# A convolution in quarter products with two transfers a pair, and attention denominators inverted once for four chunks

## What is computed

```python
x = x + L0(gn(x))      # linear attention over multi-scale heads
x = x + L1(gn(x))      # sparse plus linear attention, 4 heads of 64

def L0(x):
    qkv = conv1x1(x, w_qkv)                       # 768 channels
    agg = conv5x5_depthwise(qkv, w_dw, pad=2)
    agg = conv1x1(agg, w_pw, groups=96)           # mixes 8 channels of a head
    ms = concat([qkv, agg])                       # 64 heads of (q, k, v), 8 channels each
    q, k = relu(q), relu(k);  v = [v, 1]
    kv = einsum('bgnd,bgne->bgde', k, v)
    out = einsum('bgnd,bgde->bgne', q, kv)
    out = out[..., :-1] / (out[..., -1:] + 1e-15) # the denominators
    return conv1x1(out, w_proj)
```

## Time and profile before

| | |
|---|---|
| median of 3 runs | 9082.88 us (9064.64 to 9105.43) |
| the profiled execution's own time | 9057.69 us |
| its span | 9055.9 us |
| PE, PE weight load | 84%, 57% of the span busy |
| DVE, ACT, POOL | 56%, 39%, 42% |
| mean granted clock of PE | 0.919 of full |

### The profile page before, as it was taken

One profiled execution on the slowest core, in us unless ns is written; L12 is line 12 of the kernel. 1 busy time (PEld: TensorE's weight loads), 2 busy tenths in 40 slices (PEclk: granted clock), 3 DMA queues, 4 the chain that ended last, 5 costly groups with the idle time before them and its releaser, 6 DMA issues.

```text
span 9055.9 us, 206227 instructions
## 1 busy us (share of the span) xinstructions
PE 7636.7 (84%) x65004; PEld 5190.5 (57%) x65004; DVE 5037.9 (56%) x11563; ACT 3520.5 (39%) x9207; POOL 3786.7 (42%) x10084
## 2 busy tenths in 40 slices
PE   8978799787997879978899778997789977799788
PEld 5655556555565555655555555565555555566555
DVE  3475644756447564475644756447564475644655
ACT  1145621445214552145521455215552155511555
POOL 2345533445334553345533444334443344533444
PEclk9988999888999889988999888998889988999888
DMA  3201122011220112201122111221112211122111
GB/s 101 65 16 26 41 87 65 16 26 38 89 65 16 27 42 85 65 18 26 51 75 65 21 22 49 77 65 21 23 53 73 65 22 22 57 68 65 24 20 55
DMA packets 398743, 431.90 MB, mean 48 GB/s; under 512 B 159184, under 2 KB 355984, under 8 KB 393296
## 3 DMA queue, kind: packets, MB, share of 16 engines
q1 hardware_dynamic: 397648, 418.42, 16.3%
HBM read 102.76 MB, written 67.63 MB: 19 GB/s over the span
## 4 chain that ended last, share of the span: by engine, by line
PE 54%; DVE 23%; issue 7%; DMA 6%; ACT 5%; DVEq 3%; SPq 1%; POOL 0%; ACTq 0%; POOLq 0%
PE PS L623 12%; PE PS L686 7%; DVE arena L1144 5%; PE PS L913 5%; DVE arena L1234 4%; PE PS L778 3%; PE PS L666 3%; PE PS L878 3%; PE PS L838 3%; PE PS L847 3%; DVE SM L1379 3%; ACT arena L1088 3%; DVEq L1367 2%; DMA kv_rows<-arena 2%; PE PS L654 2%
## 5 line engine op out<-in xcount | busy, mean ns | idle before, releaser
L982 ACT ACTIVATE arena<-PS 128x128 f32<-128x128 f32 (+5 forms) x4160 | 1552.0, 399 | 1947.5 <-PE PS L623 596.5
L561 POOL COPY arena<-arena 64x129 f32 x6144 | 1527.9, 291 | 1372.0 <-PE PS L884 1094.0
L485 POOL TENSOR_TENSOR arena<-arena 128x512 f32<-128x512 f32 x768 | 806.2, 1072 | 1459.5 <-PE PS L623 1443.6
L623 PE MATMUL PS<-arena 128*128 128x256 f32 x6144 | 1359.1, 379 | 46.4 <-DMA arena<-arena 46.3
L1144 DVE COPY arena<-PS 64x260 f32<-64x260 f32 (+2 forms) x1272 | 634.3, 515 | 1352.5 <-PE PS L623 524.7
L623 PEld LDWEIGHTS PS<-arena 128*128 128x128 f32 x6144 | 1155.4, 189 | 270.6 <-issue 98.0
L1144 DVE COPY arena<-arena 64x129 f32 x4096 | 840.9, 267 | 398.3 <-PE PS L884 285.9
L1234 DVE RECIPROCAL arena<-arena 128x512 f32<-128x512 f32 x256 | 857.5, 3350 | 119.1 <-ACT arena L1030 117.5
L818 PE MATMUL PS<-arena 64*64 64x192 f32 x8192 | 699.0, 386 | 256.9 <-POOL arena L561 242.0
L491 POOL TENSOR_TENSOR BUF<-BUF,arena 128x512 f32<-128x512 f32 x256 | 358.2, 1399 | 1282.3 <-ACT arena L1018 1282.3
L1379 DVE TENSOR_REDUCE SM<-PS 128x1 f32<-128x384 f32 x1024 | 570.6, 558 | 539.7 <-issue 434.3
(11 more groups left out here) (102 smaller groups left out, 10563.4 us busy)
## 6 DMA issues: line engine op xcount, KB each, us to landing
arena<-arena SPq DMA_DIRECT2D x1024, 128.0 KB, 2.3
arena<-arena SPq DMA_DIRECT2D x768, 144.5 KB
BUF<-in_x SPq DMA_DIRECT2D x18, 2048.0 KB, 12.0
kv_rows<-arena SPq DMA_DIRECT2D x256, 130.0 KB, 3.5
arena<-kv_rows SPq DMA_DIRECT2D x256, 130.0 KB
out<-BUF SPq DMA_DIRECT2D x64, 512.0 KB, 2.6
arena<-in_taps SPq DMA_DIRECT2D x96, 288.0 KB, 3.6
W<-in_w SPq DMA_DIRECT2D x2, 768.0 KB, 5.8
```

What stands on the lines that cost most here:

```text
L485: last = pool.tensor_tensor(o, tap, mix, ALU.mult)
L561: last = pool.tensor_copy(G[p % GD][0:D, j // 3, j % 3, :], KVB[0:D, bass.ds(off, KVW)])
L623: last = nc.tensor.matmul(bank(i)[:, a * 256:(a + 1) * 256], lhsT=TW[n % 2][:, a * CH + k * P:a * CH + (k + 1) * P], rhs=src[:, k // 2:k / ...
L982: return nc.scalar.activation(o, i, ACT.Copy)
```

## The change

The convolution goes from 16 planes of 16x16 to PL = 8 planes (fy 4, fx 2) of 16 rows x 32 columns, PAD = 17*34. One head's matrix is then 64x64 at SHIFTS = 6 shifts, and a pair is done in quarters of PE's array: rows by the head a, columns by the output half o (8 rows of the plane). So a pair is 24 matmuls of 64x64x256 where it was 8 of 128x128x256. Head a of a pair has an item of its own, with the output half o in partitions 64*o; a pair takes two items, one for ACT, one for DVE, each read out in two copies of 64x256. A pair is loaded in one DMA (289 KB, from 16 partitions) and stored in one (256 KB, to 16 partitions), one pair later in SP's order than before (k >= 3). POOL builds the matrices with one multiplication of 128x384, and the taps are 224 columns where they were 576. All planes of x and RAW are now read with a stride of two elements instead of four, in rows of 32.

In the second attention the denominators are no longer spread at once. Four chunks' denominators are made by matmuls with the weights WDC (128x32) into the four 32-partition strips of one bank (6, 7); ACT copies the bank (128x512) to DNP, DVE inverts it once for the four chunks, both quads ahead of the first chunk; then from_head, a matmul with 32 rows, spreads each chunk's strip to a bank, which ACT copies to DN as before. Chunks are attended and projected by twos. The first attention stays as it was.

```diff
-PL, R = 16, 16
-PW = R + 1
-PAD = PW * PW
+PL, R, RC2 = 8, 16, 32
+PW, PC = R + 1, RC2 + 2
+PAD = PW * PC
+SHIFTS = 6
...
-    return g * HALF_ITEMS + (I_CQ + m + 8 if m < 0 else I_CKV + m + 2 * max(0, (m - 2) // 2))
+    return g * HALF_ITEMS + (I_CQ + 2 * (m + 8) if m < 0 else I_CKV + 2 * m + 2 * max(0, (m - 2) // 2))
...
-                        for a in range(2):
-                            sp.dma_start(IN[n % 3][:, a * PAD:(a + 1) * PAD],
-                                         head_rows(RAW[j], 2 * pr + a).rearrange("p (f n) -> p f n", f=PL)
-                                         ).then_inc(s_in[n % 3], 16)
+                        sp.dma_start(IN[n % 3], pair_rows(RAW[j], pr).rearrange("p (f n) -> p f n", f=PL)
+                                     ).then_inc(s_in[n % 3], 16)
...
-                        sp.wait_ge(s_free[i % 2], b * IT + 2 + count(i, i % 2))
-                        for a in range(2):
-                            sp.dma_start(head_rows(AGG[j], 2 * pr + a).rearrange("p (f n) -> p f n", f=PL),
-                                         OUTG[n % 3][:, a * 256:(a + 1) * 256]).then_inc(s_og[n % 3], 16)
+                        sp.wait_ge(s_free[0], b * IT + 2 + count(i, 0))
+                        settle(sp)
+                        sp.wait_ge(s_free[1], b * IT + 2 + count(i + 1, 1))
+                        sp.dma_start(pair_rows(AGG[j], pr).rearrange("p (f n) -> p f n", f=PL),
+                                     OUTG[n % 3]).then_inc(s_og[n % 3], 16)
...
                                 claim(i)
+                                claim(i + 1)
                                 pe.wait_ge(s_tw, b * PAIRS + n + 1)
...
-                                for a in range(2):
-                                    src = IN[n % 3][:, a * PAD:(a + 1) * PAD].rearrange("p (r c) -> p r c", r=PW)
-                                    for k in range(4):
+                                for k in range(SHIFTS):
+                                    for a, o in ((0, 0), (1, 1), (0, 1), (1, 0)):
+                                        head = slice(a * D, (a + 1) * D)
+                                        rows = IN[n % 3][head, :].rearrange("p (r c) -> p r c", r=PW)
+                                        y, xx = k // 3 + o * R // 2, k % 3
                                         last = nc.tensor.matmul(
-                                            bank(i)[:, a * 256:(a + 1) * 256],
-                                            lhsT=TW[n % 2][:, a * CH + k * P:a * CH + (k + 1) * P],
-                                            rhs=src[:, k // 2:k // 2 + R, k % 2:k % 2 + R],
-                                            start=(k == 0), stop=(k == 3))
-                                hand(i, last)
+                                            bank(i + a)[o * D:(o + 1) * D, 0:256],
+                                            lhsT=TW[n % 2][head, k * D:(k + 1) * D],
+                                            rhs=rows[:, y:y + R // 2, xx:xx + RC2],
+                                            start=(k == 0), stop=(k == SHIFTS - 1))
+                                        if k == SHIFTS - 1 and o != a:
+                                            hand(i + a, last)
...
+                        def head_denominators(quad):
+                            for r in range(4):
+                                last = nc.tensor.matmul(PS[32 * r:32 * r + 32, 6 + quad, :], lhsT=WDC,
+                                                        rhs=q_chunk(4 * quad + r), start=True, stop=True)
+                            last.then_inc(s_den, 1)
+
+                        def attend_pair(c):
+                            for k in (c, c + 1):
+                                i = base + att_item(1, k) + 1
+                                claim(i)
+                                hand(i, nc.tensor.matmul(bank(i), lhsT=WN[1], rhs=q_chunk(k), start=True, stop=True))
+                            pe.wait_ge(s_dnr, 2 * (b * 2 + g) + c // 4 + 1)
+                            for k in (c, c + 1):
+                                claim(base + att_item(1, k))
+                            settle(pe)
+                            for k in (c, c + 1):
+                                i, rows = base + att_item(1, k), slice(32 * (k % 4), 32 * (k % 4) + 32)
+                                hand(i, nc.tensor.matmul(bank(i), lhsT=from_head[rows, :], rhs=DNP[c // 4][rows, :],
+                                                         start=True, stop=True))
...
+                        for quad in range(2):
+                            head_denominators(quad)
+                        for c in range(0, NCH + 2, 2):
                             if c < NCH:
-                                attend(1, c)
+                                attend_pair(c)
                             if c >= 2:
...
+                                project(c - 2)
+                                project(c - 1)
...
-                    i = conv_item(n)
-                    if i % 2 == e:
-                        wait_filled(eng, b, i)
-                        eng.wait_ge(s_og[n % 3], b * 512 + 32 * (n // 3 + 1))
-                        op(OUTG[n % 3], PS[:, i % 4, :]).then_inc(s_free[e], 1)
+                    i = conv_item(n) + e
+                    wait_filled(eng, b, i)
+                    eng.wait_ge(s_og[n % 3], b * 256 + 16 * (n // 3 + 1))
+                    op(OUTG[n % 3][e * D:(e + 1) * D, 0:256], PS[0:D, i % 4, 0:256])
+                    op(OUTG[n % 3][e * D:(e + 1) * D, 256:512], PS[D:P, i % 4, 0:256]).then_inc(s_free[e], 1)
...
+                            for quad in range(2 * src):
+                                dve.wait_ge(s_dnc, 2 * (b * 2 + g) + quad + 1)
+                                nc.vector.reciprocal(DNP[quad], DNP[quad]).then_inc(s_dnr, 1)
...
-                            order.after(nc.vector.reciprocal(DN[c % 2], DN[c % 2]))
+                            if src == 0:
+                                order.after(nc.vector.reciprocal(DN[c % 2], DN[c % 2]))
```

More of the change, by code:

```diff
@@ L55 @@
 PAIRS = 48
-TAPS = 72
+TAPS = 8 * SHIFTS + 8
 TP = 16
@@ L959, in empty_half @@
             weights(1)
[L960 to L964 removed]
+            for c in range(0, NCH + 2, 2):
+                for k in (c, c + 1):
+                    if c < NCH:
+                        attend(1, k)
+                for k in (c - 2, c - 1):
+                    if c >= 2:
+                        project(k)
         def x_chunk(X, i):
```

149 lines of the change are left out of this document (81 added, 68 removed).

## The result

The changed kernel takes **8999.18 us** (median of 4 runs, 8992.83 to 9017.64) beside 9076.40 us (9064.64 to 9105.43) of the kernel before on the same chip: a ratio of 0.9914, 95% interval 0.9885 to 0.9942. It is faster by 77 us where 164 us were forecast, inside the stated range. The profiled execution took 9017.64 us, its span is 9015.8 us and its mean granted clock 0.904 (before 0.919).

A forecast was written before the change was run, and what follows sets the result against it. PE was taken as the bound, with DVE setting the end in g = 1. Terms -10.9 - 10.4 + 0.8 + 2.8 - 2.8 = -20.5 us an image, -164 us over eight: 8919 us, range 8810 to 9060.

The forecast's parts named there:

- first 12 pairs: Convolution at the start of a half: 12 x 2.80 = 33.6 us for 44.52 and 44.01.
- six periods: Convolution pairs with first attention between: pair B waits for DVE to free banks; 52.2 us for 51.8, +0.4 a half.
- rest and kv: Stage behind the convolution, 25.26 us: two reciprocals on DVE set the pace and stay, so 0.
- last stage g = 0: Second attention and projection, first half: +1.0 us from waits for two reciprocals, 1.75 us of lost clock, in sum +2.8.
- last stage g = 1 with what is behind PE: Second half: 48.9 us on PE, then DVE's last addition and six moments; 54.8 us for 57.56, -2.8.
- A pair on PE: Convolution pair as 12 rounds of four quarters at once: 2.80 us for 3.46, ends 2.68 and 3.08.
- Feeding it: Convolution loads by DMA: each has two pairs, 5.6 us, to land; costed at nothing.
- the DMA rival: The 186 GB/s plateau stays in the first 12 pairs, 3.0 us a pair: +2.4 a half, 8957 us; chance 0.12.
- Q: Time of one convolution pair, taken as 2.80 us; 0.1 us of it is 29 us in all.
- the sign of being wrong: Signs named: a pair over 3.3 us, clock well below 1.00 mid-convolution, or last stage over 50 us in g = 0.
- the 322 us of DVE's time: Second attention: 96 reciprocals leave, 6 a half, worth 322 us on DVE, nearly all lost in waits of PE's.
- The clock's rival: PE at the 1.2 GHz level throughout the attention's periods: +5.9 in each of 96, +570 us, 9490 us; chance 0.07.

The follow-up runs named there:

- run 1: Changed kernel with the second attention back in its old form, the convolution in quarters kept; 8958.44 us, ratio to the kernel before 0.9857.
- run 2: Kernel before with only the second attention's new form added, the convolution as before; 9146.35 us, ratio to the kernel before 1.0082.
- run 9: Changed kernel with a pair's loads and stores both on 16 partitions at a step of 7 (other channels than the reference); 8984.69 us, single time.
- run 10: Changed kernel with PE's two bank claims of a pair placed behind its waits for taps and load; 8948.65 us, single time.
- run 5: Changed kernel with the first attention's denominators and numerators in banks 6 and 7, the convolution in banks 0 to 3; 8780.86 us, ratio 0.9680.
- run 4: Changed kernel with four unread matmuls a half added in PE's idles of the second attention; 8943.30 us, ratio to the kernel before 0.9853.
- run 3: Changed kernel with the second quad's reciprocal moved behind the division of chunk 1 on DVE; 8960.40 us, ratio to the kernel before 0.9869.

## Why the prediction was off

Two steps of the forecast failed by their size. The last stage was charged 1.75 us of lost clock a half where 5.6 and 4.5 us were lost, and a period of the attention 8.7 us where it takes 9.1. Together they are 9.3 of the 11.2 us an image by which the first block's sum misses. The accounts of one image, forecast and measured (means over eight, the table above):

| term | forecast | measured |
|---|---|---|
| first 12 pairs, two halves | -10.9, -10.4 | -10.1, -10.1 |
| six periods, two halves | +0.4, +0.4 | +2.5, +2.6 |
| rest and kv | 0, 0 | +0.5, +0.3 |
| last stage g = 0 | +2.8 | +6.5 |
| last stage g = 1 with what is behind PE | -2.8 | -1.5 |
| sum | -20.5 | -9.3 |

The first block's 475.2 us became 466.7 (-8.5, 0.8 of it back in stages not listed); eight of these are 68 us. In the profiled pair of executions 29 us came back in the second block, hence 40 us less span; the medians, 77 us apart, sit on the other side of 68.

Runs 1 and 2 part the miss by what was changed. For the convolution and its planes the forecast has -21.7 us an image (-10.9, -10.4, +0.8 and -1.2 for the moments), and run 1 shows -19.4. For the second attention it has +1.2 (+2.8 in g = 0, -1.6 in g = 1 without the moments' stride), and it costs 9.5 (run 2) to 10.9 (the change less run 1). So the convolution was forecast well, and the second attention was not.

1. **A pair on PE: too dear.** 2.61 us, below the lower end of 2.68. The 0.08 us over in the earlier trace rows does not come again in a stream of 192 records. The Trainium skill (TensorE: Matmul & The Clock Gate, Measured speedup vs the span model) has its 3.07 times for four tiles of 32 rows; the estimate of 3.4 us from it did not show: for these quarters it is four times (10.4 us one after the other, 2.61).
2. **Feeding it: "I cost it at nothing" was wrong.** Some 3.5 us a half are idles for loads, the DMA rival in mechanism: it has 3.0 us a pair, and 35.0 us are 2.9. But its limit, a plateau of 186 GB/s, was one microsecond of a stage whose mean was 164, with PE as its bound, and so no limit. With Q 0.19 too high in 12 pairs (2.3 us) the two errors nearly cancel: that 33.6 against 35.0 is a small miss is luck. Part of these idles stood in the rows: the 1.26 us of the earlier trace rows lie ahead of the fifth pair, and before the change PE waited 1.3 us there and as much ahead of the ninth in the mean of 16 halves; their loads are the ones behind the taps in SP's order. The forecast let both waits vanish, and both are still there (run 9). The row I leaned on, 0.83 and 235 GB/s, had a transfer over 128 partitions in it and said nothing of one over 16. The Trainium skill (DMA: Bandwidth & Descriptors, how many engines a DMA uses) let more engines be expected at 16 partitions, and the share did go from 0.52 to 0.88; the bytes followed in part, from 164 to 196 GB/s.
3. **The periods: right mechanism, wrong size.** PE's wait for DVE's multiplication decides them, at the place named. The term mis-sized is 5.9 us to pair B's start, which is 6.4: 0.3 of it is PE's way through the waits behind the claim (run 10), the rest ACT's and DVE's later starts. Six times that, less the shorter pair, is the difference of 2.1 us a half. The larger omission: I priced this wait at +0.4 a half where "the PE work alone would promise -8" and did not ask what else it cost. Removing it gives 11.0 us a half (run 5).
4. **The last stage, g = 0: the clock was mis-sized.** Without lost clock the forecast was 47.1, and the stage with PE kept busy takes 48.1 (run 4). I charged 1.75 us, read from the stage behind the convolution, where PE's work is small matmuls after one idle. Here two idles stand 1.1 us apart (3593.05 to 3594.17), and the low level (1.2 GHz) lasts 13.6 us in six of eight images: 5.6 us lost in the mean. Runs 3 and 4 show the idles to be the cause, by two ways that leave each other's part alone: every execution with both idles in full loses 2.8 to 5.6 us, run 3 loses 1.3 and 1.7, run 4 nothing. The stage came out above 50 us, the sign of being wrong that the forecast had named.
5. **g = 1: DVE gave more, PE less.** The moments cost 0.61, below the 0.68 I had as the end, and the additions 0.69; so what is behind PE is 9.8 us for 12.5. PE's end came at 51.5 instead of 48.9, for the clock again. What g = 1 gained comes with the planes' stride, not with fewer reciprocals: run 1 keeps all the reciprocals and is shorter still. The forecast "nearly all of it is lost in waits of PE's" (the 322 us of DVE's time) held, and understated it: the part alone makes the kernel slower (run 2).
6. **The clock's rival** was put in the wrong place. In the periods an idle of 1.66 us leaves the clock at 1.00; it fell in the last stage, which had it in the forecast at a third of its size.

## What to carry to other kernels

When PE's work shrinks by a quarter inside a rotation of shared buffers, recount who hands the buffers back: here a wait on four shared banks ate 176 us, more than twice what the whole change gained, and banks that were free would have given it. A reciprocal saved where DVE has time is worth nothing (g = 0 here), and one moved ahead of the first consumer costs PE's idle time plus the clock that the idle takes down; time each part of a change alone before adding them. Where a stream is close to what DMA can bring, look at landing times, at GB/s over a whole stage and at what each load waits for in its queue, not at the share of busy engines.

## What the runs showed of the hardware

- Quarters of the array (64x64) with 256 columns of float32 run four at a time with no cost over: 0.217 us a round, 192 records long.
- Two row strips of a bank-filling matmul do run together (L732: four records of 512 columns in 1.13 us), and so do four strips of 32 columns (L717: 16 in 1.92).
- PE at the 1.2 GHz level for 13.65 us from within the second of two idles, 1.42 and 2.54 us, and at full clock through idles of 1.57 to 1.75 us once in 9 us. With 1.42 and 1.47 most of the loss is gone (1.3 us an image for 5.6), and with work in the idles all of it.
- The 16 DMA engines moved 196 GB/s at a share of 0.88 with 16 partitions at a step of 4, and 156 GB/s at a share of 0.90 with the loads from 16 adjacent ones.
- Waits already met, placed behind a late one in PE's program, cost 0.3 us a period (54.6 to 52.9 us for six).
- DVE's moments over rows of 32 at a stride of two elements take 0.61 to 0.64 us for 512 elements (1.07 at a stride of four): no slower than unstrided ones, 0.68.
